# A small vision tower: recurrence on the centred stream, gates on 32 rows, third norm's gamma and beta folded into weights

## The chip, the cores and the metric

One core of a Trainium2 chip (trn2). The time is that of the whole program on the device, in microseconds (us). It is the median of several runs; each run's time lies within a few tenths of a microsecond of the others. TensorE multiplies matrices, VectorE, ScalarE and GpSimd work on tiles in on-chip memory, and SyncE queues most transfers. GpSimd doesn't read the accumulator memory (PSUM) that TensorE writes.

## The reference

16 images of 96 x 96 x 3 are cut into 6 x 6 patches (36 positions, 576 tokens of 64 channels) and pass four layers, each with a mixing block and an expert block. Each block's output is added to the stream and normalised. Cut to what the change touches:

```
h = layernorm(h + block0_attention(h)); h = layernorm(h + block0_experts(h))

# layer 1: a linear recurrence over the 36 positions, complex, per image
u     = h @ (B * exp(gamma_log)[:, None]).T          # complex
s[t]  = lambda * s[t-1] + u[t]
h     = layernorm(h + (s @ C.T).real)

# layer 1 experts: all 8 evaluated, the best two of the router's logits weighted
for e in 8: out += combine[:, e] * (gelu(h @ w1[e] + b1[e]) @ w2[e] + b2[e])

# layer 2: top-8 attention with scores max_d(q_d + k_d), then experts:
xn     = layernorm(h) * gamma + beta                 # a norm of the expert block's own
logits = xn @ Wr + br                                # best two, softmax over them
for e in 8: y += w[:, e] * (gelu(xn @ W1[e] + b1[e]) @ W2[e] + b2[e])
```

The last layer (attention, one shared hidden layer, eight output matrices, a final norm) is not changed in what it computes.

## The kernel before

The program is written by hand: one instruction list for each engine, with semaphores between them. There is no planner; each engine does its instructions in the order in which they stand, so an instruction that waits holds up all behind it on its engine. The stream of 576 tokens lies as 128 x 288: rows 0 to 63 hold the 64 channels of the first 288 tokens (h = 0), rows 64 to 127 those of the second 288 (h = 1). Most steps run once for each half, on 64 rows of the array.

Each norm is the same sequence. TensorE adds the block's output to the centred residual in bank YB. ScalarE squares it (L1025), VectorE copies it to `centred` (XC, L1259), TensorE forms the variances (L481), ScalarE takes the root (L1030), VectorE the reciprocal (L1262, `RS`). TensorE turns and broadcasts the reciprocals over the rows (`broadcast`, L489, called in `spread`), VectorE multiplies `centred` by them into `h` (HP) in `normalise` (L1267). `idle(n, bank)` (L474) issues n products of 512 columns on zeros, whose result nobody reads; they stand where TensorE would wait.

Recurrence (TensorE L779 to L794, VectorE L1494 to L1511): `h` is projected by `lru_b1` and `lru_b2` to two banks each (L784), VectorE multiplies both by tables of cosines and sines (L1505, L1507), adds them (L1508), scans (L1509) and rotates back (L1510, L1511); TensorE projects the result into YB (L792).

Experts with all eight evaluated (layers 1 and 2), `ffn(n, src)`: `up` projects a chunk of 128 hidden columns for both halves (L521), ScalarE applies gelu with the bias (L1045), `gate` spreads the chunk's routing weight over the 128 rows by a 0/1 selector (L528), VectorE multiplies (L1339), `down` projects back (L534), and a bias product adds the output biases (L540). Layer 1 has four chunks of two experts each, layer 2 eight. The routing weights stand in bf16 in `combine_parts_T` (CT3): 64 rows, of which 0 to 31 hold the three exact parts and the mark of eight experts for h = 0, and 32 to 63 those for h = 1. Rows 64 to 127 are zero. A gate product reads all 128 rows; its selector is zero for the other half.

Selection in layer 2's attention: VectorE finds the eight best keys of each query (`topped`), replaces them by a mark (L1573, `replaced`) and masks the probabilities with it (L1578, `prob2`); TensorE turns these (L877). In between TensorE runs three blocks of seven idle products: after `late_keys_in`, after `topped` and after `top_sum`, and one after `replaced`. GpSimd subtracts and scales (L446, L453), ScalarE takes exponentials (L1147) and then loads its square-root table (L1037).

Layer 2's own norm: the reciprocals of both norms are broadcast (L489, 24 passes), two idle products follow, VectorE normalises into `xn` (L1595) and multiplies by gamma and adds beta (L1596); `ffn(2, XN)` waits for that. The router uses weights already multiplied by gamma.

## Time and profile before

| | us |
|---|---|
| median of 3 runs | 147.52 (147.13 to 147.79) |
| the profiled execution, its own time | 147.68 |
| its span, first to last instruction | 145.9 |
| TensorE busy with products (PE) | 132.4 |
| VectorE busy | 95.1 |
| ScalarE busy | 66.1 |
| GpSimd busy | 44.3 |

In the profile PE is TensorE's products, PEld its weight loads, DVE VectorE, ACT ScalarE, POOL GpSimd. L784 is line 784 of the kernel. A product in fp32 shows as two passes (two records), one in bf16 as one. "128*64 128x288" is a product on 128 rows and 64 columns of the array, streaming 288 columns. A length of a product includes the time in which the next one has already started; distances between starts tell how long the array is taken.

### The profile page before, as it was taken

To read this page: it belongs to the slowest core of one execution; us is meant where nothing else is said; L and a number is where in the kernel's file an instruction comes from. 1 tells how busy PE (TensorE), PEld (TensorE's weight loads), DVE (VectorE), ACT (ScalarE), POOL (GpSimd) and SP (SyncE) were. 2 spreads that over 40 slices of the span, in tenths; PEclk is the share of its full clock that TensorE was granted. 3 is DMA by queue.
4 is the path that set the end of the run, shared out by engine and by line. 5 is a ranking of instruction groups with operands and counts; after the bars stand their busy time and mean duration, and the time that the engine had idled before them with its cause. 6 is when DMAs were issued, how large, how long until landed. Compare 5 with 4: busy or idle time off the path is not lost.

```text
span 145.9 us, 2995 instructions
## 1 busy us (share of the span) xinstructions
PE 132.4 (91%) x1159; PEld 72.9 (50%) x1159; DVE 95.1 (65%) x301; ACT 66.1 (45%) x142; POOL 44.3 (30%) x99
## 2 busy tenths in 40 slices
PE   6999999989998996899999869998999999999960
PEld 2444566647963542554553324663454465554640
DVE  6506757799953386666778999629467477306991
ACT  3555780377601101691443006365860555568352
POOL 8819887579740000036000034000592000000000
PEclk9999999999999999999999999999999999999999
DMA  4999992000000000000020000000000000000001
GB/s 158 346 401 354 244 355 119 0 4 0 4 0 0 0 4 0 0 2 0 9 56 0 0 2 4 0 0 4 0 0 0 0 4 0 0 4 0 2 0 41
DMA packets 3830, 7.74 MB, mean 53 GB/s; under 512 B 1596, under 2 KB 1820, under 8 KB 3816
## 3 DMA queue, kind: packets, MB, share of 16 engines
q1 hardware_dynamic: 3504, 7.44, 15.5%
q8 instruction: 9, 0.15, 0.4%
q10 hardware_dynamic: 312, 0.11, 0.3%
q14 instruction: 5, 0.04, 0.1%
HBM read 7.18 MB, written 0.15 MB: 50 GB/s over the span
## 4 chain that ended last, share of the span: by engine, by line
PE 69%; DVE 23%; ACT 4%; issue 3%; DVEq 0%; ACTq 0%
PE ps L474 12%; PE ps L534 5%; PE ps L521 4%; PE ps L481 4%; PE ps L489 4%; DVE scores L1552 3%; PE ps L648 3%; DVE residual L1673 3%; PE ps L528 2%; DVE patch_sb L1665 2%; PE ps L503 2%; PE ps L693 2%; PE ps L701 2%; PE ps L605 2%; PE ps L637 2%
## 5 line engine op out<-in xcount | busy, mean ns | idle before, releaser
L474 PE MATMUL ps<-idle_operand 128*128 128x512 bf16 x123 | 34.1, 393 | 3.2 <-DVE scores L1552 1.6
L1037 ACT ACT_TABLE_LOAD x16 | 20.5, 1283 | 0.3
L474 PEld LDWEIGHTS ps<-idle_operand 128*128 128x128 bf16 x123 | 10.4, 102 | 16.9 <-issue 3.7
L1025 ACT ACTIVATE squares<-ps 128x288 f32<-128x288 f32 x7 | 2.9, 411 | 23.8 <-PE ps L792 8.4
L381 POOL CAST combine_parts_T<-combine_parts_T 64x288 f32<-64x288 bf16 x2 | 0.8, 418 | 36.7 <-DVE combine_parts_T L1287 36.7
L1259 DVE COPY centred<-ps 128x288 f32<-128x288 f32 x7 | 3.2, 456 | 11.9 <-ACT squares L1025 11.9
L1339 DVE TENSOR_TENSOR hidden_gated<-hidden,ps 128x576 f32<-128x576 f32 x12 | 8.4, 750 | 3.3 <-PE ps L528 3.3
L976 PE MATMUL ps<-weights_sb,hidden 128*128 128x256 f32 (+2 forms) x28 | 9.8, 472 | 0.0
L1045 ACT ACTIVATE hidden<-ps,weights_sb 128x576 f32<-128x576 f32 x12 | 8.5, 738 | 2.5 <-PE ps L521 2.1
L1552 DVE TENSOR_REDUCE scores<-ps 128x32 f32<-128x512 f32 (+1 forms) x13 | 7.7, 653 | 0.7 <-PE ps L844 0.7
L446 POOL TENSOR_TENSOR patch_sb<-scores,top 128x288 f32<-128x288 f32 (+1 forms) x2 | 1.6, 782 | 18.2 <-DVE top L1561 18.1
L534 PE MATMUL ps<-hidden_gated,weights_sb 128*64 128x288 f32 x48 | 6.9, 417 | 0.0
L481 PEld LDWEIGHTS ps<-consts_sb,squares 128*96 128x96 f32 x48 | 4.7, 164 | 3.9 <-ACT squares L1025 3.4
L489 PE MATMUL ps<-consts_sb,rstd 96*64 96x96 f32 x108 | 6.2, 253 | 0.1
L489 PEld LDWEIGHTS ps<-consts_sb,rstd 96*64 96x64 f32 x108 | 4.7, 136 | 2.7 <-DVE rstd L1262 2.0
L521 PE MATMUL ps<-xn,weights_sb 64*128 64x288 f32 x32 | 5.5, 446 | 0.5 <-ACT hidden L1045 0.4
L976 PEld LDWEIGHTS ps<-weights_sb,hidden 128*128 128x128 f32 (+1 forms) x28 | 4.6, 182 | 2.4 <-issue 1.6
L481 PE MATMUL ps<-consts_sb,squares 128*96 128x2 f32 x48 | 5.4, 228 | 0.1
L503 PE MATMUL ps<-h,consts_sb 128*128 128x288 f32 x14 | 5.2, 451 | 0.0
L840 PE MATMUL ps<-bconsts_sb,q_parts 128*128 128x512 bf16 (+1 forms) x13 | 4.8, 369 | 0.0
L1267 DVE TENSOR_TENSOR h<-centred,ps 128x288 f32<-128x288 f32 x6 | 2.7, 448 | 3.1 <-PE ps L489 3.1
L1262 DVE RECIPROCAL rstd<-std 96x6 f32<-96x6 f32 (+1 forms) x8 | 1.5, 192 | 4.6 <-ACT std L1030 4.6
(346 smaller groups left out, 281.1 us busy)
## 6 DMA issues: line engine op xcount, KB each, us to landing
patch_sb<-patches SPq DMA_DIRECT2D x6, 288.0 KB, 4.8
weights_sb<-weights SPq DMA_DIRECT2D x1, 717.0 KB, 14.0
weights_sb<-weights SPq DMA_DIRECT2D x1, 689.0 KB, 12.7
weights_sb<-weights SPq DMA_DIRECT2D x1, 640.0 KB, 6.8
weights_sb<-weights SPq DMA_DIRECT2D x1, 532.0 KB, 7.5
weights_sb<-weights SPq DMA_DIRECT2D x1, 512.0 KB, 10.3
weights_sb<-weights SPq DMA_DIRECT2D x1, 394.0 KB, 11.3
selectors<-sels SPq DMA_DIRECT2D x1, 384.0 KB, 9.8
```

What stands on the lines that cost most here:

```text
L474: mm(PS[:, bank, :], idle_in[:, 0:P], idle_in[:, :], start=True, stop=True)
L481: last = mm(psVar[:, 2 * t:2 * t + 2], SQ[:, cols(t)], c("mean"), start=True, stop=True)
L489: last = mm(dst[rows(h), cols(t)], RS[:, at + 2 * t + h:at + 2 * t + h + 1].to_broadcast([TT, D]), c("ident", TT)[:, 0:TT], start=True, st ...
L503: mm(psY, c(name), HP[:, :], start=True, stop=stop, skip_group_check=True)
L521: last = mm(PS[:, z + h, 0:HALF], w1[rows(h), ch, :], src[rows(h), :], start=True, stop=True)
L534: last = mm(PS[rows(h), YB, 0:HALF], w2[:, ch, :], HG[:, ch % GRING, h, :], start=False, stop=(ch == chunks - 1), skip_group_check=True)
L840: mm(out.rearrange("p (s e) -> p s e", e=D), QA[:, j * P:(j + 1) * P], cb("id2").unsqueeze(1).to_broadcast([P, keys, D]), start=True, stop ...
L976: return mm(y3(q, a, b), tok3(q, ch), wd[:, ch, a * E:b * E], start=False, stop=(ch == 1), skip_group_check=True)
L1037: act.activation(warm[:, tables[0]:tables[0] + 1], warm[:, 0:1], func)
L1045: act.activation(HR[:, at % RING, :, :], two(ZA if ch % 2 == 0 else ZB), func, bias=w(f"b1_{n}")[:, ch:ch + 1]).then_inc(S["act_out"], 1)
L1339: dve.tensor_tensor(HG[:, at % GRING, :, :], HR[:, at % RING, :, :], two(GATE_AT[n][ch]), ALU.mult)\
L1552: dve.tensor_reduce(SC[:, j, :, 8 * g:8 * g + keys].rearrange("p h s -> p s h"), PS[:, n % 4, 0:keys * D].rearrange("p (s h d) -> p s h d" ...
```

## The change

Three parts, and a renaming.

1. Recurrence. The projections read `centred` instead of `h`, straight after the variance products. The reciprocals are then broadcast to all 128 rows for each half (banks G and G+1). ScalarE copies the two parts that belong to `centred` to on-chip memory (into `KS`), and GpSimd forms `h` from them. VectorE no longer normalises here; it multiplies the rotated sum by the reciprocals (128 x 576) before the scan. The idle products stand 6 before and 4 after the residual product instead of 9 after it.
2. Gates. Each half's gate product reads only its own 32 rows of selector and routing weights.
3. Fold. beta times the first expert weights is formed by eight products of one column (on 64 rows) between the idle products of the selection, 4 before and 3 after instead of 7. ScalarE copies the result, GpSimd adds it to the bias and multiplies the weights `w1_2` (128 x 1024) by gamma. VectorE's multiplication by gamma and addition of beta goes.
4. Some semaphores of one use each are merged (`q_mid` and `q_low`, `x3_ready` and `h3_copied`, `logits3_in` and `hres_in`), with the counts adjusted.

```diff
@@ gpsimd
+            pool.wait_ge(S["xc"], 3)
+            pool.wait_ge(S["rstd_lru"], 2)
+            pool.tensor_tensor(HP[:, :], XC[:, :], KS[:, 0:HALF], ALU.mult).then_inc(S["hp"], 1)
             gates32(1)
...
+            pool.wait_ge(S["fold2_in"], 1)
+            pool.tensor_tensor(B12[:, :], B12M[:, :], w("b1_2"), ALU.add).then_inc(S["folded2"], 1)
+            pool.wait_ge(S["folded2"], 1)
+            pool.tensor_scalar(w("w1_2"), w("w1_2"), w("gam2"), None, ALU.mult).then_inc(S["folded2"], 1)
             gates32(2)
@@ tensor, gate
                     for h in range(2):
-                        last = mm(PS[:, bank + h, 0:HALF], sel[:, g, h, :], CT3[:, :], start=True, stop=True)
+                        at = slice(4 * E * h, 4 * E * (h + 1))
+                        last = mm(PS[:, bank + h, 0:HALF], sel[at, g, h, :], CT3[at, :], start=True, stop=True)
@@ tensor, recurrence
             variance(2)
-            spread(2)
             pe.wait_ge(S["w_r1"], 16)
-            pe.wait_ge(S["hp"], 3)
+            pe.wait_ge(S["xc"], 3)
             for bank, name in ((ZA, "lru_b1"), (ZB, "lru_b2")):
                 for h in range(2):
-                    last = mm(PS[:, bank + h, 0:HALF], w(name)[rows(h), :], HP[rows(h), :], start=True, stop=True)
+                    last = mm(PS[:, bank + h, 0:HALF], w(name)[rows(h), :], XC[rows(h), :], start=True, stop=True)
                 last.then_inc(S["lru_u"], 1)
+            pe.wait_ge(S["rs"], 3)
+            for h in range(2):
+                for t in range(NT):
+                    last = mm(PS[:, G + h, cols(t)], RS[:, 2 * t + h:2 * t + h + 1].to_broadcast([TT, P]),
+                              c("ident", TT)[:, 0:TT], start=True, stop=True)
+            last.then_inc(S["bc"], 1)
             pe.wait_ge(S["cen_c"], 1)
+            idle(6, MB)
+            pe.wait_ge(S["hp"], 3)
             residual("ident")
-            idle(9, MB)
+            idle(4, MB)
@@ tensor, selection
             pe.wait_ge(S["topped"], QT * HEADS)
-            idle(7, MB)
+            idle(4, MB)
+            pe.wait_ge(S["v2_ready"], 4)
+            for ch in range(E):
+                last = mm(PS[:, G, ch:ch + 1], w("w1_2", 64)[:, ch * P:(ch + 1) * P], w("bet2", 64), start=True, stop=True)
+            last.then_inc(S["fold2_mm"], 1)
+            idle(3, MB)
...
             pe.wait_ge(S["xn"], 2)
+            pe.wait_ge(S["folded2"], 2)
             ffn(2, XN)
@@ scalar
+            act.wait_ge(S["bc"], 3)
+            for h in range(2):
+                act.activation(KS[rows(h), 0:HALF], PS[rows(h), G + h, 0:HALF], ACT.Copy).then_inc(S["rstd_lru"], 1)
...
+            act.wait_ge(S["fold2_mm"], 1)
+            act.activation(B12M[:, :], PS[:, G, 0:E], ACT.Copy).then_inc(S["fold2_in"], 1)
             table(ACT.Sqrt)
...
+            act.wait_ge(S["folded2"], 1)
             hidden(2, ACT.Gelu, range(1))
@@ vector
             variance(2)
-            normalise(2, HP[:, :], "hp")
...
             link(dve.tensor_tensor(ua[:, :], ua[:, :], ub[:, :], ALU.add))
+            dve.wait_ge(S["rstd_lru"], 2)
+            link(dve.tensor_tensor(ua[:, :].rearrange("p (h n) -> p h n", h=2), ua[:, :].rearrange("p (h n) -> p h n", h=2),
+                                   two(G), ALU.mult))
             link(dve.tensor_tensor_scan(wst[:, :], rr[:, :], ua[:, :], 0.0, ALU.mult, ALU.add))
...
-            link(dve.tensor_tensor(XN[:, :], XC[:, :], psBC2, ALU.mult))
-            dve.tensor_scalar(XN[:, :], XN[:, :], w("gam2"), w("bet2"), ALU.mult, ALU.add).then_inc(S["xn"], 1)
+            dve.tensor_tensor(XN[:, :], XC[:, :], psBC2, ALU.mult).then_inc(S["xn"], 1)
```

## Rows read from the trace of the kernel before

**Rows 1.** The page: span, busy time, granted clock, and shares of the chain

```profile
span 145.9 us, 2995 instructions
...
PE 132.4 (91%) x1159; PEld 72.9 (50%) x1159; DVE 95.1 (65%) x301; ACT 66.1 (45%) x142; POOL 44.3 (30%) x99
...
PEclk9999999999999999999999999999999999999999
...
PE 69%; DVE 23%; ACT 4%; issue 3%; DVEq 0%; ACTq 0%
```

**Rows 2.** Timeline, 48-56 us (start, length, engine, line, operation, count, [idle before])

```profile
48.01 0.46 DVE L1259 COPY centred<-ps 128x288 f32<-128x288 f32 x1 [1.29 <-ACT squares L1025]
...
48.02 0.58 PEld L481 LDWEIGHTS ps<-consts_sb,squares 128*96 128x96 f32 x6 [0.56 <-ACT squares L1025]
...
48.56 0.81 PE L474 MATMUL ps<-idle_operand 128*128 128x512 bf16 x3
...
49.29 0.53 PEld L489 LDWEIGHTS ps<-consts_sb,rstd 96*64 96x64 f32 x12 [0.42 <-DVE rstd L1262]
...
50.06 0.45 DVE L1267 TENSOR_TENSOR h<-centred,ps 128x288 f32<-128x288 f32 x1 [0.84 <-PE ps L489]
...
50.66 1.24 PE L784 MATMUL ps<-h,weights_sb 64*128 64x288 f32 x8
...
51.52 0.76 DVE L1505 TENSOR_TENSOR lru_ua<-ps,rot_in_c 128x576 f32<-128x576 f32 x1 [1.01 <-PE ps L784]
...
52.98 0.76 DVE L1508 TENSOR_TENSOR lru_ua<-lru_ua,lru_ub 128x576 f32<-128x576 f32 x1
...
53.77 1.36 DVE L1509 TENSOR_TENSOR_SCAN lru_state<-decay,lru_ua 128x576 f32<-128x576 f32 x1
...
55.98 0.71 PE L792 MATMUL ps<-lru_wc,weights_sb 128*64 128x288 f32 x4 [1.45 <-DVE lru_wc L1510]
```

**Rows 3.** The same view of TensorE's weight loads, columns of 128

```profile
36.12 1.86 PEld L626 LDWEIGHTS ps<-x_slots,weights_sb 64*128 64x128 f32 x32
...
90.62 1.07 PEld L877 LDWEIGHTS ps<-consts_sb,probs 128*128 128x128 f32 x10 [0.27 <-DVE probs L1578]
```

**Rows 4.** Timeline, 94 us, ScalarE: a copy of 128x288

```profile
94.20 0.41 ACT L1152 ACTIVATE ctx_sb<-ps 128x288 f32<-128x288 f32 x1 [1.52 <-PE ps L888]
```

**Rows 5.** Groups of GpSimd by line and form (| busy, mean ns)

```profile
L411 POOL TENSOR_SCALAR decay<-decay,lru_par 128x576 f32<-128x576 f32 x1 | 1.7, 1719 | 0.0
...
L453 POOL TENSOR_TENSOR patch_sb<-patch_sb,row_stat 128x288 f32<-128x288 f32 x1 | 0.7, 672 | 0.6 <-DVE row_stat L1571 0.6
```

**Rows 6.** The chain that ended last, 106-109 us (start, length, engine, line, count)

```profile
106.32 0.49 PE ps L528 x4
...
106.81 0.48 PE ps L540 x2
...
108.66 0.60 PE ps L528 x4
```

**Rows 7.** Timeline, first expert stage, VectorE's gate multiplications

```profile
64.91 2.75 DVE L1339 TENSOR_TENSOR hidden_gated<-hidden,ps 128x576 f32<-128x576 f32 x4 [0.70 <-PE ps L528]
```

**Rows 8.** Timeline, 98-99 us: idle products, scale by gamma, first up products

```profile
98.49 0.60 PE L474 MATMUL ps<-idle_operand 128*128 128x512 bf16 x2
...
98.61 0.43 DVE L1596 TENSOR_SCALAR xn<-xn,weights_sb 128x288 f32<-128x288 f32 x1
...
99.09 1.24 PE L521 MATMUL ps<-xn,weights_sb 64*128 64x288 f32 x8
```

**Rows 9.** Timeline of TensorE, 88-92 us: idle products and transposes

```profile
88.22 1.89 PE L474 MATMUL ps<-idle_operand 128*128 128x512 bf16 x8
...
90.26 0.39 PE L474 MATMUL ps<-idle_operand 128*128 128x512 bf16 x1 [0.16 <-DVE scores_rest L1573]
...
90.63 1.31 PE L877 MATMUL ps<-consts_sb,probs 128*128 128x128 f32 x10
```

**Rows 10.** Timeline, 92.7 us: the context's short products

```profile
92.73 1.41 PE L888 MATMUL ps<-probs_T,v_blockdiag 128*32 128x40 f32 x64
```

More of the change, by code:

```diff
@@ L96 @@
 guarded
-lru_u lru_w
-k_done q_done v2_done q_hi q_rest q_mid q_low q_parts k_parts k_bcast v2_ready score_mm score_red late_keys late_keys_in top_in top_out top_sum sub2 exp2_out norm2
+lru_u lru_w rstd_lru
+k_done q_done v2_done q_hi q_rest q_act q_parts k_parts k_bcast v2_ready score_mm score_red late_keys late_keys_in top_in top_out top_sum sub2 exp2_out norm2
 prob2 prob2_t prob2_copied ctx2_done ctx2_ready
-x3_done x3_ready s3_done h3_t h3_copied exp3_in exp3_out p3_ready p3_t p3_copied0 p3_copied1
-h3_ready y3_done comb3_done wd_c logits3_T logits3_in bias3 bias3_c bias3_split hres hres_in tile3 ss
+x3_done s3_done h3_t third_in exp3_in exp3_out p3_ready p3_t p3_copied0 p3_copied1
+fold2_mm fold2_in folded2
+h3_ready y3_done comb3_done wd_c logits3_T bias3 bias3_c bias3_split hres turned3_in tile3 ss
 out_act out_dve stored""".split()
@@ L215, in tower @@
         CX = sb("ctx2_sb", [P, HALF])
+        B12, B12M = sb("b1_2_folded", [P, E]), sb("b1_2_beta", [P, E])
         XT = sb("x3_T", [P, HALF])
@@ L829, in _ @@
             idle(6, ZA + 1)
-            pe.wait_ge(S["q_low"], 1)
+            pe.wait_ge(S["q_act"], 2)
             pe.wait_ge(S["q_parts"], 1)
@@ L919, in _ @@
             residual("ident")
-            pe.wait_ge(S["x3_ready"], 1)
+            pe.wait_ge(S["third_in"], 1)
             for h in range(2):
@@ L928, in _ @@
             idle(10, ZB)
-            pe.wait_ge(S["h3_copied"], 1)
+            pe.wait_ge(S["third_in"], 2)
             for h in range(2):
@@ L994, in _ @@
             part(0, 0)
-            pe.wait_ge(S["logits3_in"], 1)
+            pe.wait_ge(S["turned3_in"], 1)
             mm(PS[:, G + 1, E:FT * E].rearrange("p (g e) -> p g e", e=E), LT[:, 0:P],
@@ L1045, in hidden @@
                     act.activation(HR[:, at % RING, :, :], two(ZA if ch % 2 == 0 else ZB), func,
-                                   bias=w(f"b1_{n}")[:, ch:ch + 1]).then_inc(S["act_out"], 1)
+                                   bias=(B12 if n == 2 else w(f"b1_{n}"))[:, ch:ch + 1]).then_inc(S["act_out"], 1)
             act.wait_ge(S["tok_w"], 16)
@@ L1130, in _ @@
             act.wait_ge(S["q_rest"], 1)
-            act.activation(q2b[:, :], qres[0:64, :], ACT.Copy).then_inc(S["q_mid"], 1)
-            act.activation(QA[64:128, :], qres[64:128, :], ACT.Copy).then_inc(S["q_low"], 1)
+            act.activation(q2b[:, :], qres[0:64, :], ACT.Copy).then_inc(S["q_act"], 1)
+            act.activation(QA[64:128, :], qres[64:128, :], ACT.Copy).then_inc(S["q_act"], 1)
             act.wait_ge(S["v2_done"], 1)
@@ L1169, in _ @@
             act.wait_ge(S["x3_done"], 1)
-            act.activation(XT[:, :], PS[:, ZB, 0:HALF], ACT.Copy).then_inc(S["x3_ready"], 1)
+            act.activation(XT[:, :], PS[:, ZB, 0:HALF], ACT.Copy).then_inc(S["third_in"], 1)
             act.wait_ge(S["h3_t"], 1)
             act.activation(HB[:, :, :].rearrange("p b d -> p (b d)"), flat2(G, PER * P, POS), ACT.Copy)\
-               .then_inc(S["h3_copied"], 1)
+               .then_inc(S["third_in"], 1)
             for h in range(2):
@@ L1192, in _ @@
             act.wait_ge(S["logits3_T"], 1)
-            act.activation(LT[:, :], PS[:, MB, 0:P + 64], ACT.Copy).then_inc(S["logits3_in"], 1)
+            act.activation(LT[:, :], PS[:, MB, 0:P + 64], ACT.Copy).then_inc(S["turned3_in"], 1)
             table(ACT.Exp)
@@ L1197, in _ @@
             act.wait_ge(S["hres"], 1)
-            act.activation(YM[0:64, 0, :, E], PS[0:64, YB, 0:D], ACT.Copy).then_inc(S["hres_in"], 1)
+            act.activation(YM[0:64, 0, :, E], PS[0:64, YB, 0:D], ACT.Copy).then_inc(S["turned3_in"], 1)
             act.activation(YM[:, 1:FT, :, E].rearrange("p (h b) d -> p h b d", b=2),
                            PS[:, YB, D:D + 2 * P].rearrange("p (b h d) -> p h b d", b=2, h=2), ACT.Copy)\
-               .then_inc(S["hres_in"], 1)
+               .then_inc(S["turned3_in"], 1)
             table(ACT.Sqrt)
@@ L1543, in _ @@
             dve.tensor_tensor(slots(qres), psQ, slots(QA), ALU.subtract).then_inc(S["q_rest"], 1)
-            dve.wait_ge(S["q_mid"], 1)
+            dve.wait_ge(S["q_act"], 1)
             dve.tensor_tensor(QB[0:64, 0:QT * P], qres[0:64, :], q2b[:, :], ALU.subtract).then_inc(S["q_parts"], 1)
@@ L1670, in summed3 @@
                 p = rows3(q)
-                dve.wait_ge(S["hres_in"], 1 if q == 0 else 2)
+                dve.wait_ge(S["turned3_in"], 2 if q == 0 else 3)
                 sync()
```

## The prediction, made before the changed kernel had run

> **What bounds the kernel now.** I read three views. The page first: TensorE is busy for 91% of the 145.9 us and holds 69% of the chain that ended last, VectorE 23% [rows 1]. That doesn't mean that TensorE work costs time one for one: many of its products are idle ones on zeros that only fill waits (`idle` in the code). So for each of the three stretches that the change touches I read the timeline, to see which wait ends last there, and the chain of waits, whose pieces give the distance from one product's start to the next. Nothing else in the kernel moves; the renamed semaphores wait for the same instructions as before.
>
> **1. Recurrence (46.8 to 57.3 us).** Before, everything hangs in one line: centred copy until 48.47, square root and reciprocal, broadcast of the reciprocals from 49.29, normalise on VectorE 50.06 to 50.51, projections from 50.66, rotation from 51.52, its sum at 52.98, scan at 53.77 [rows 2].
> Afterwards the projections wait only for the centred copy (48.47) and for the six variance products ahead of them. Those run from 48.02 to 48.56, when idle products follow [rows 2], and a change of array shape costs about 0.10 (priced in part 2). So the projections start at 48.65, 2.01 earlier, and rotation and its sum follow 2.01 earlier: rotation 49.51, sum 50.97 to 51.73. VectorE's reciprocal is done by 49.29 and isn't in their way.
> But the scale by the reciprocals now comes after the rotation, and its own line is longer. The broadcast is queued behind the projections, which hold TensorE until 49.71. It also loads 128 columns of weights instead of 64, so its 12 passes no longer run in two halves of the array at once. Loads of 128 columns in fp32 come 1.07/10 = 0.107 apart in one place and, in two row halves at once, 1.86/32 x 2 = 0.116 per half in another [rows 3]; I take 0.11. That is 49.71 + 0.10 for the shape + 0.10 for the first load + 12 x 0.11 = 51.2 us. The result is taken up about 0.2 later, as now (loads end at 49.82, normalise starts at 50.06 [rows 2]). ScalarE's two copies have 288 columns each, like the copy of 0.41 us in [rows 4]. They start about 0.35 apart: 51.4 + 0.35 + 0.41 = 52.17. VectorE, free since 51.73, waits until 52.22, multiplies (0.76, 0.79 with its link, like the sum of the same size [rows 2]) and scans at 53.01 instead of 53.77. **Gain 0.76.** Bounds: if the copies cost nothing beyond VectorE's own order, the scan starts at 51.73 + 0.05 + 0.79 = 52.57, a gain of 1.2. If the loads cost 0.13 and the copies run end to end, 0.4.
> The normalised stream for the residual moves to GpSimd: 0.67 for 128x288 [rows 5], 52.22 to 52.9. TensorE runs six idle products meanwhile, then the residual (0.6) and four more idle ones of 0.215 (0.9), so it is ready near 54.5, before the first rotated state comes (55.98 - 0.76, [rows 2]). Free; the cover is 0.7 us.
>
> **2. Gates on 32 rows.** A gate is now two products of 288 columns in bf16 one after the other, 0.49/4 = 0.122 each [rows 6]. Afterwards each half reads only its own 32 rows. In the projections two products on separate halves of 64 rows already run side by side: eight fp32 passes of 288 columns in 1.24 us, 0.155 each, while the bias product's two on the full array take 0.48, 0.24 each [rows 2, 6]. So a pair should take 0.13 instead of 0.24: 0.12 saved.
> Against it stands the change of array shape. Four gates between other full-array products take 0.49; between down products, which use 64 columns, 0.60 [rows 6]. A change of shape is therefore about 0.10. Today the gates share the full-array shape with the residual and with the bias product. On 32 rows they don't, so residual to gate, gate to bias and bias to gate are new changes.
> The Trainium skill says the same against this change: "Mode switching requires drain" (TensorEngine Tiling (Array Packing), Tiling Modes). By that page alone every gate of a stage would be bracketed by two pauses; the rows give each of them a price, 0.10.
> First expert stage: the first gate starts 0.10 later and its pair is 0.12 shorter. VectorE then multiplies four times without a pause [rows 7] and sets the rest, so the gain is 0.02.
> Second expert stage, along TensorE's queue [rows 6]: gate 1 is done 0.02 earlier. Gate 2 saves 0.12, bias and gate 3 lose 0.10 + 0.10 and gain 0.12, so the down products start 0.04 late. Gates 4 and 5 save 0.12 each at an unchanged number of shape changes: 0.08 earlier after gate 4, 0.20 at the next down products, 0.32 when gate 6 is done. From there VectorE's last two multiplications and the last down product follow. **Gain 0.31 here, 0.33 in all.** Bounds: a loss of 0.4 if the pairs don't overlap (four new changes of shape on the path and nothing saved), a gain of 0.5 if the changes cost half.
>
> **3. Gamma and beta folded.** Removed: one VectorE instruction of 0.43 ahead of the third stage [rows 8]. It hides less than its length. Without it the stream is ready when that one begins now, 98.6, but TensorE's two idle products start at 98.49 and last until 98.93, and with the change of shape the first up product can't start before 99.03. It starts at 99.09 now. Gain 0.06. The router behind it comes 0.43 earlier, but its result is picked up by TensorE only after the fifth up product, so this brings nothing.
> Added: eight fp32 products of one column on 64 rows, between the idle products of the selection. Here the idle products are not free filler. Eight of them take 1.89 us from 88.22 on, of which the last alone shows 0.39: (1.89 - 0.39)/7 = 0.215 apart, so TensorE has no pause until 88.22 + 8 x 0.215 = 89.94 [rows 9]. The next event is at 90.26, when VectorE's replacements are done, and the transposes start at 90.63 [rows 9]. The slack is 0.32, plus 0.15 because the last idle product needn't wait.
> An fp32 product is two passes with a load each. For a single column the load sets the pace: the six variance passes, 96 columns loaded for 2 streamed, take (48.56 - 48.02)/6 = 0.09 each, the first being dearest [rows 2]. In proportion that is 0.12 for 128 columns, and rows 3 give 0.107 and 0.116. I take 0.112. All eight use the same 64 rows, so none run side by side: 16 x 0.112 = 1.79, plus two changes of shape, 0.19. The idle products stay seven in number (4 + 3), so these 1.98 us come on top: the second block now ends at 89.94 + 1.98 = 91.92, the single idle product at 92.15, and the transposes start there instead of at 90.63. That is 1.52 late; their first load is no longer exposed, which gives about 0.03 back. **Loss 1.49, net of the gain above 1.43.** Probabilities, context, output projection and everything behind follow one another from the transposes, so nothing takes it up. Bounds: 1.8 if a pass costs 0.13. The shortest rows of products show 64 in 1.41 us, 0.022 each, on four column groups [rows 10]; at that the block costs 0.35 + 0.19 and the loss is near zero.
> The copy on ScalarE delays its table load and square-root warm-up to about 91.7; its next work, the copy of the probabilities, comes after 93. GpSimd scales 1024 columns: 1.72 us for 576 [rows 5] makes 3.1, from about 90.6 to 93.7, while the first up product comes near 100.5, so 6 us of cover. All free.
>
> **Sum.** -0.76 - 0.33 + 1.43 = +0.34. The profiled execution took 147.68, 1.78 more than its span, and stands 0.16 above the median of 147.52, inside the runs' spread. 147.52 + 0.34 = 147.86.
>
> **Rivals.** (a) The fold is nearly free: short products run at the pace of [rows 10], the late transposes vanish. For it: those rows, and TensorE looks idle here. Against it: the variance passes, with two columns, already cost 0.09. Then -0.76 - 0.33 + 0 - 0.06 = -1.15: 146.4. 12%. The Trainium skill (TensorEngine Tiling (Array Packing), Instruction Overhead) would have it so: a product with a free dimension of 1 has the latency of one with 60, about 60 cycles. By that page 16 passes are an estimate of 0.4 us and the loss of part 3 is about nothing; the rows of the variance speak against it. (b) Slower: pairs on 32 rows run one after the other. No row here shows products on 32 rows. Price: +0.1 in the first expert stage and +0.3 in the second instead of -0.33, decided by whether two starts of one pair lie 0.12 or under 0.02 apart. 147.86 + 0.73 = 148.6. 14%. (c) The recurrence brings what VectorE alone allows, 1.2: 147.4. 10%. (d) The stretch of one-column products lets the granted clock fall; the page shows full clock throughout [rows 1], through a TensorE pause of 1.45 us too [rows 2]. The eleven idle products behind would cost 0.22 more each: 150.2. 3%.
>
> **Chances.** Forecast 61%, its own range 147.3 to 148.4. The range reaches from 146.8 to 148.7, which takes in (b), (c) and most mixtures and leaves out (a) and (d). A difference of 0.5% (0.74 us) is about what this kernel's measurement can tell: faster 0.14, within 0.60, slower 0.26.
>
> **What would show it.** Projections 2 us earlier but the scan only 0.6 to 0.9 earlier, with VectorE waiting for ScalarE's copies; pair starts within 0.02 and a pause of 0.1 around each pair; 16 passes some 0.11 apart near 88 us and transposes waiting for nothing but TensorE's queue. It is wrong if the passes come under 0.05 apart, or if the transposes still wait for VectorE.

## The result, and the profile after

The changed kernel takes 147.70 us (median of 22 runs, 147.04 to 150.29) against 147.12 for the kernel before, timed beside it (22 runs, 146.66 to 147.94). The ratio is 1.0035, 95% interval 1.0019 to 1.0051: 0.5 us slower. The interval lies above 1, so the sign is clear, and the size is 0.35%. The ratios here leave out two executions far above the rest of their kernel, 150.29 us of the changed kernel and 153.21 us of e8.

The page of the changed kernel, to be read against [rows 1]:

```profile
span 145.6 us, 3027 instructions
...
PE 133.1 (91%) x1171; PEld 74.0 (51%) x1171; DVE 94.7 (65%) x300; ACT 67.1 (46%) x145; POOL 49.0 (34%) x102
...
PEclk9999999999999999999999999999999999999999
...
PE 72%; DVE 18%; ACT 5%; issue 2%; DVEq 0%; ACTq 0%
```

VectorE's share of the chain fell from 23% to 18% and TensorE's rose from 69% to 72%. Most of this is the selection: there the chain ran over VectorE until 21.75 us behind the fifth square, and now it passes to TensorE's own queue at 18.41 (below). The span is 0.3 us shorter than before's although the median is 0.6 longer. The two profiled executions differ by 0.6 us before the third norm, where nothing was changed. So spans are no measure here. I compare the distances between ScalarE's squares, which open every norm. Before, as the timeline of ScalarE has them (start, length, engine, line, operation):

```profile
47.56 0.41 ACT L1025 ACTIVATE squares<-ps 128x288 f32<-128x288 f32 x1 [1.45 <-PE ps L775]
...
68.47 0.41 ACT L1023 ACTIVATE squares<-ps 128x288 f32<-128x288 f32 x1 [2.53 <-PE ps L534]
95.45 0.41 ACT L1025 ACTIVATE squares<-ps 128x288 f32<-128x288 f32 x1 [0.84 <-PE ps L894]
113.11 0.41 ACT L1025 ACTIVATE squares<-ps 128x288 f32<-128x288 f32 x1 [5.10 <-PE ps L534]
```

and the same rows of the changed kernel:

```profile
46.95 0.41 ACT L1048 ACTIVATE squares<-ps 128x288 f32<-128x288 f32 x1 [1.46 <-PE ps L785]
...
67.12 0.41 ACT L1046 ACTIVATE squares<-ps 128x288 f32<-128x288 f32 x1 [2.63 <-PE ps L544]
95.58 0.41 ACT L1048 ACTIVATE squares<-ps 128x288 f32<-128x288 f32 x1 [0.84 <-PE ps L916]
112.85 0.41 ACT L1048 ACTIVATE squares<-ps 128x288 f32<-128x288 f32 x1 [4.82 <-PE ps L544]
```

These are the third, fifth, sixth and seventh of eight squares. From the third on there are five distances (68.47 - 47.56 is two of them, 9.83 and 11.07), and behind the last square the tail, to the start of the last instruction; together they are all of the program that the change touches. I read the same rows for every experiment:

| us | recurrence | first experts | attention 2 | second experts | layer 3 | tail | sum less before's | ratio, 95% interval |
|---|---|---|---|---|---|---|---|---|
| before | 9.83 | 11.07 | 26.99 | 17.66 | 11.18 | 21.54 | | |
| after | 9.20 | 10.97 | 28.46 | 17.27 | 11.19 | 21.56 | +0.38 | 1.0035 (1.0019 to 1.0051) |
| e1 recurrence only | 9.20 | 10.98 | 27.00 | 17.65 | 11.18 | 21.90 | -0.36 | 0.9982 (0.9958 to 1.0006) |
| e2 gates only | 9.83 | 11.05 | 27.01 | 17.31 | 11.19 | 21.57 | -0.31 | 0.9962 (0.9941 to 0.9982) |
| e3 fold only | 9.83 | 11.07 | 28.46 | 17.61 | 11.19 | 21.54 | +1.43 | 1.0129 (1.0092 to 1.0165) |
| e4 no filler | 9.20 | 10.97 | 28.09 | 17.27 | 11.19 | 21.56 | +0.01 | 0.9961 (0.9932 to 0.9990) |
| e5 fold early | 9.20 | 10.97 | 27.61 | 17.27 | 11.19 | 21.56 | -0.47 | 0.9939 (0.9913 to 0.9965) |
| e6 scale before copies | 9.00 | 10.97 | 28.45 | 17.27 | 11.19 | 21.54 | +0.15 | 1.0035 (1.0006 to 1.0063) |
| e7 bias behind gates | 9.20 | 10.97 | 29.00 | 17.16 | 11.19 | 21.55 | +0.80 | one run, 147.23 us |
| e8 fold twice | 9.20 | 10.97 | 31.93 | 17.27 | 11.19 | 21.54 | +3.83 | 1.0268 (1.0233 to 1.0303) |
| f1 no fold | 9.20 | 10.96 | 27.06 | 17.31 | 11.19 | 21.91 | -0.64 | 0.9960 (0.9940 to 0.9979) |
| f2 no fold, ordered | 9.01 | 10.95 | 26.97 | 17.21 | 11.19 | 21.91 | -1.03 | 0.9944 (0.9919 to 0.9968) |
| f3 all, ordered | 9.00 | 10.96 | 26.98 | 17.17 | 11.18 | 21.56 | -1.42 | 0.9917 (0.9891 to 0.9943) |
| g1 f2, one fewer on VectorE | 9.01 | 10.96 | 27.35 | 17.20 | 11.19 | 21.55 | -1.01 | 0.9900 (0.9865 to 0.9936) |

What was changed repeats to 0.02 us in the profiles. The times of one kernel spread by 0.8 us and more all the same. One source is seen in the attention column: in some executions the score products wait for the transfer of the keys and start 0.4 to 0.6 us later (e5, e7, g1; shown at e5). The sums come from one execution of each kernel. For the changed kernel +0.38 lies inside the interval of the times (+0.28 to +0.75 us).

**Where the time went.** Timeline of the changed kernel in the recurrence (against [rows 2]):

```profile
47.39 0.46 DVE L1290 COPY centred<-ps 128x288 f32<-128x288 f32 x1 [1.29 <-ACT squares L1048]
...
48.01 1.24 PE L793 MATMUL ps<-centred,weights_sb 64*128 64x288 f32 x8
...
49.18 1.41 PEld L798 LDWEIGHTS ps<-consts_sb,rstd 96*128 96x128 f32 x12 [0.38 <-issue]
...
50.80 0.83 ACT L1141 ACTIVATE ks<-ps 64x288 f32<-64x288 f32 x2 [2.41 <-PE ps L798]
51.73 0.76 DVE L1540 TENSOR_TENSOR lru_ua<-lru_ua,ps 128x576 f32<-128x576 f32 x1 [0.64 <-ACT ks L1141]
51.78 0.80 POOL L439 TENSOR_TENSOR h<-centred,ks 128x288 f32<-128x288 f32 x1 [10.79 <-ACT ks L1141]
52.52 1.36 DVE L1542 TENSOR_TENSOR_SCAN lru_state<-decay,lru_ua 128x576 f32<-128x576 f32 x1
```

This execution stands 0.61 us earlier than before's. From the third square the projections start 1.06 us later instead of 3.10, 2.04 earlier; the scan starts 5.57 later instead of 6.21, only 0.64 earlier. The 0.64 us in which VectorE waits for the copies is the wait that took the place of the one removed. The chain has the second of the two copies by itself:

```profile
51.23 0.41 ACT ks L1141
```

The chain of waits of the changed kernel through the fold (start, length, engine, line, count), against [rows 9]:

```profile
85.58 1.04 PE ps L483 x4
86.62 1.87 PE ps L887 x16
88.49 2.48 PE ps L483 x11
90.97 1.11 PE ps L899 x10
```

Idle products, the sixteen one-column passes, eleven more idle products, transposes: TensorE's own queue without a gap. Before, the transposes waited for VectorE; now VectorE is done 1.2 us before they start.

### The profile page after: what moved, and what is told of

It is laid out like the page before. It is cut to its first block, busy times and chain, and to the rows that moved or that the text cites. A ratio compares the mean times of both kernels' runs of the same rounds, so it can differ in the third digit from the quotient of the medians.

```text
span 145.6 us, 3027 instructions
## 1 busy us (share of the span) xinstructions
PE 133.1 (91%) x1171; PEld 74.0 (51%) x1171; DVE 94.7 (65%) x300; ACT 67.1 (46%) x145; POOL 49.0 (34%) x102
## 4 chain that ended last, share of the span: by engine, by line
PE 72%; DVE 18%; ACT 5%; issue 2%; DVEq 0%; ACTq 0%
PE ps L483 14%; PE ps L544 5%; PE ps L530 4%; PE ps L490 4%; PE ps L498 3%; DVE scores L1585 3%; PE ps L658 3%; DVE residual L1705 3%; DVE patch_sb L1697 2%; PE ps L512 2%; PE ps L711 2%; PE ps L615 2%; PE ps L703 2%; PE ps L647 2%; PE ps L538 2%
## 5 line engine op out<-in xcount | busy, mean ns | idle before, releaser
L483 PE MATMUL ps<-idle_operand 128*128 128x512 bf16 x119 | 33.1, 393 | 3.0 <-DVE scores L1585 1.6
L1068 ACT ACTIVATE hidden<-ps,b_folded 128x576 f32<-128x576 f32 x8 | 5.8, 739 | 2.0 <-PE ps L530 1.7
L498 PE MATMUL ps<-consts_sb,rstd 96*64 96x96 f32 x96 | 5.5, 253 | 0.1
L498 PEld LDWEIGHTS ps<-consts_sb,rstd 96*64 96x64 f32 x96 | 4.2, 136 | 2.3 <-DVE rstd L1293 1.7
L1053 ACT ACTIVATE std<-ps,eps 96x6 f32<-96x6 f32 x8 | 2.1, 261 | 5.3 <-PE ps L490 5.3
```

The lines of the kernel that those rows point to most:

```text
L483: mm(PS[:, bank, :], idle_in[:, 0:P], idle_in[:, :], start=True, stop=True)
L498: last = mm(dst[rows(h), cols(t)], RS[:, at + 2 * t + h:at + 2 * t + h + 1].to_broadcast([TT, D]), c("ident", TT)[:, 0:TT], start=True, st ...
L1068: act.activation(HR[:, at % RING, :, :], two(ZA if ch % 2 == 0 else ZB), func, bias=(B12 if n == 2 else w(f"b1_{n}"))[:, ch:ch + 1]).then_ ...
```

## The experiments

**One part at a time.** e1 is the kernel before with the recurrence's lines of the diff alone, e2 with the gates' alone, e3 with the fold's alone. All three have the merged semaphores of part 4 as well.

```diff
 e1, against before: tensor; copies, GpSimd's product and the scaling as in part 1
-            spread(2)
...
-                    last = mm(PS[:, bank + h, 0:HALF], w(name)[rows(h), :], HP[rows(h), :], start=True, stop=True)
+                    last = mm(PS[:, bank + h, 0:HALF], w(name)[rows(h), :], XC[rows(h), :], start=True, stop=True)

 e2, against before
+                        at = slice(4 * E * h, 4 * E * (h + 1))
-                        last = mm(PS[:, bank + h, 0:HALF], sel[:, g, h, :], CT3[:, :], start=True, stop=True)
+                        last = mm(PS[:, bank + h, 0:HALF], sel[at, g, h, :], CT3[at, :], start=True, stop=True)

 e3, against before: tensor; bias and scaling of the weights as in part 3
-            idle(7, MB)
+            idle(4, MB)
+            pe.wait_ge(S["v2_ready"], 4)
+            for ch in range(E):
+                last = mm(PS[:, G, ch:ch + 1], w("w1_2", 64)[:, ch * P:(ch + 1) * P], w("bet2", 64), start=True, stop=True)
+            last.then_inc(S["fold2_mm"], 1)
+            idle(3, MB)
```

> Only the recurrence part of the change; gates and fold as before. My theory (the broadcast of 12 passes and the two copies set the time of the scan): 0.64 us less than before, as the two traces show from the square ahead to the square behind (9.84 and 9.20); ratio 0.9957. Rival 1 (the stage gains only what the six idle products around it allow, so nothing): ratio 1.000. Rival 2 (VectorE alone sets it): 1.2 us less, ratio 0.992.

> Only the gates on 32 rows. Theory (pairs side by side, 0.12 saved each, about 0.10 paid for every change of shape): 0.35 to 0.5 us less, ratio 0.997; the pair starts 0.004 apart. Rival (the changes of shape eat the gain): ratio 1.000 or above. Rival on the clock (products on 32 rows let the granted clock fall in some executions): granted clocks under 1.000 and single times 1 us above the rest here, and not in the kernels without this part.

> Only gamma and beta folded. Theory (16 passes of 0.112 and two changes of shape behind full idle products): 1.45 us more than before, ratio 1.010; transposes wait for TensorE's queue alone. Rival (the fold is free and the loss of the whole change comes from somewhere else): ratio 0.999 to 1.001. Rival on the clock (one-column products let the granted clock fall in some executions): granted clocks under 1.000 and single times 1 to 3 us above the rest here, and not in the kernels without this part.

Recurrence: -0.63 in its own stage and -0.09 in the next. Gates: -0.02 and -0.35. Fold: +1.47 before the transposes and -0.05 in its expert stage. That adds up to +0.33; the changed kernel's stages show 9.20 + 10.97 + 28.46 + 17.27 = 65.90 against 65.55, +0.35. To 0.02 us the parts are independent: they share neither a gain nor a cost. e3 has the attention stage of the changed kernel, 28.46, without the other two parts, so that loss is the fold's alone. The ratio of e1 fits its stages only once its tail is seen: 21.90 instead of 21.54. I come back to this at g1.

The -0.09 behind the recurrence has its cause on ScalarE. In before it pauses ahead of the first gelu of the stage, waiting for nothing that the profile shows; in e1 and the changed kernel it doesn't. The chains of before, and then of the changed kernel:

```profile
61.10 0.21 ACT gate_col L1120
61.30 0.14 issue
61.45 0.75 ACT hidden L1045
```

```profile
59.85 0.21 ACT gate_col L1148
60.06 0.69 ACT hidden L1068
```

Counted from the fourth square, the gelu starts 4.05 us later in before, e2 and e3, where it is the 64th record on ScalarE, and 3.85 later in every kernel with the new recurrence, whose two copies make it the 66th. Of these 0.20 us 0.09 is left at the next square. No run moves the instruction without the copies, so that its place does it is not shown.

**e4, no filler.** The one-column passes take the place of the idle products instead of coming on top.

```diff
 e4, against after
-            idle(4, MB)
             pe.wait_ge(S["v2_ready"], 4)
             for ch in range(E):
                 last = mm(PS[:, G, ch:ch + 1], ...)
             last.then_inc(S["fold2_mm"], 1)
-            idle(3, MB)
@@ after top_sum
-            idle(7, MB)
+            idle(5, MB)
```

> The whole change, but the seven idle products around the fold's products are gone and the block behind has five instead of seven. Theory (the fold costs only because idle products stand in the same queue): it runs 16 x 0.112 + 0.2 = 2.0 us where 1.5 us of idle products stood, and 0.43 less of them behind, so the transposes wait for VectorE's masked probabilities again: 1.45 us less than the changed kernel, 1.1 less than before, ratio to before 0.9925. Rival (the loss comes from GpSimd's scaling of 1024 columns, or from ScalarE's later table load, which are still there): ratio stays at 1.003. Rival on the clock (fewer idle products let it fall): some executions with a granted clock under 1.000 and a median above 147.

Ratio 0.9961, and the twelve times are in two groups: six from 145.93 to 146.38 us, six from 146.79 to 147.61, the profiled one in the second. Its windows on TensorE (stretch, busy and count, granted clock) say what separates them:

```profile
86.00:87.00 1.00, 1.00 (x12) 1.00 0.06 16
87.00:88.00 1.00, 1.00 (x6) 0.61 0.00 0
88.00:90.00 2.00, 2.00 (x7) 0.50 0.00 0
```

and its chain:

```profile
85.30 1.94 PE ps L886 x16
87.24 2.66 PE ps L483 x6
89.90 1.53 PE ps L897 x10
```

Six idle products take 2.66 us, 0.44 each, where in the changed kernel eleven take 2.48, 0.225 each. Behind a stretch of one-column passes the granted clock falls from full to half, 2.4 to 1.2 GHz. This is rival (d), which I had at 3%. The first group of times, about 1.1 us below before's as forecast, is by inference the one in which the clock holds: mean clocks of the runs are 0.991 to 1.0 there and 0.979 to 0.988 in the second. With the filler in place such executions are rare: in the changed kernel one of 22 (150.29 us at a mean clock of 0.987, all others at 0.991 or more), in e3 one of 6 (150.03 us at 0.985), in e6 none of 12. So the idle products around the passes, which look like waste in the sum, mostly keep the clock. In e5 and f3 below the passes stand between score products and 21 idle ones instead, and none of their 18 executions is under 0.991. The Trainium skill says that the array's clock is gated by how busy TensorE has been (TensorE: Matmul & The Clock Gate, What's actually happening). The trace agrees in part: the clock changes with what TensorE does, but the profile's busy share doesn't tell when. TensorE is busy throughout these windows, the one ahead of the fall (86 to 87 us, in which 12 products start) included.

**e8, fold twice.** The eight products are issued twice, with the filler as in the changed kernel.

```diff
 e8, against after
-            for ch in range(E):
+            for ch in [*range(E), *range(E)]:
```

> The whole change, but the eight products of one column are issued twice, 32 passes. Theory: 16 x 0.112 = 1.79 us more in the stage from the fourth square to the fifth, 30.25 instead of 28.46; ratio to before 1.0155 where the clock holds. On the clock: 3.6 us of one-column passes in a row. If such passes don't keep the clock up, it falls to half in most or all executions, and the idle products behind take 0.43 instead of 0.216 each: 2 us more again, ratio 1.03. If they do, there is one group of times.

The stage grows by 3.47 us. The chain has the 32 passes at 3.66 us, 0.114 each as forecast, so the passes themselves explain 1.79. The rest is the clock:

```profile
86.83 3.66 PE ps L887 x32
90.48 3.70 PE ps L483 x11
94.19 1.57 PE ps L899 x10
```

Eleven idle products take 3.70 instead of 2.48, ten transposes 1.57 instead of 1.11: 1.68 together. Five of the six times lie from 150.45 to 151.23 and one is 153.21; their mean clocks are 0.975 to 0.989. So by the mean clocks a stretch twice as long lets the clock fall in every execution, although the filler stands around it.

**e5, fold early.** The same products are moved ahead of the wait for the last scores' maxima, where TensorE paused in before, ahead of 21 idle products; the filler is whole again (7 in its old place). The pause is the 1.60 us in this row of before:

```profile
85.08 5.02 PE L474 MATMUL ps<-idle_operand 128*128 128x512 bf16 x21 [1.60 <-DVE scores L1552]
```

```diff
 e5, against after
             n = len(SCORE_UNITS)
+            pe.wait_ge(S["v2_ready"], 4)
+            for ch in range(E):
+                last = mm(PS[:, G, ch:ch + 1], ...)
+            last.then_inc(S["fold2_mm"], 1)
             pe.wait_ge(S["score_red"], n)
             pe.wait_ge(S["late_keys_in"], 1)
@@ after topped
-            idle(4, MB)
-            pe.wait_ge(S["v2_ready"], 4)
...
-            last.then_inc(S["fold2_mm"], 1)
-            idle(3, MB)
+            idle(7, MB)
```

> The whole change, with the fold's eight products moved: they stand behind the last score product, where TensorE otherwise pauses for VectorE, and all three blocks of seven idle products are back. Theory (the loss is nothing but the place in TensorE's queue): 1.9 us of passes fit in the 1.99 us from the last score product to the first idle one, less 0.22 for that product itself, so the idle block starts 0.33 late and ends when VectorE's eight best keys are done; the stage from the fourth square to the fifth goes from 28.46 back to 27.0 us; ratio to before 0.9925 (1.1 less). The clock should hold as in the kernel before, so no second group of times as with the idle products taken away. Rival (one-column passes cost the clock wherever they stand, because the pause of 1.6 us is now beside them): a second group of times some 1.3 us higher, as without the idle products. Rival (GpSimd's or ScalarE's part of the fold costs): the stage stays above 28.

Ratio 0.9939, one group of times, mean clocks 0.991 or more. The timeline of TensorE has the passes under cover, and the transposes behind VectorE's last replacement again:

```profile
82.41 1.94 PE L882 MATMUL ps<-weights_sb 64*128 64x1 f32 x16
84.28 4.82 PE L483 MATMUL ps<-idle_operand 128*128 128x512 bf16 x21
89.26 0.39 PE L483 MATMUL ps<-idle_operand 128*128 128x512 bf16 x1 [0.15 <-DVE scores_rest L1605]
89.62 1.31 PE L898 MATMUL ps<-consts_sb,probs 128*128 128x128 f32 x10
```

The stage is 27.61 though, not 27.0. The missing 0.6 lies ahead of all this, in the chain of waits of the same kernel:

```profile
72.06 3.51 DMA k_parts_img<-k_parts_tok
```

The score products wait for the keys' transfer. In before and after its place in the chain is taken by idle products on TensorE. e7, whose code is the changed kernel's up to there, has the same piece of DMA (3.45 us) and the same 0.5 us, so it is a matter of the execution and not of the edit. From the first score product that reads the keys to the transposes it is 13.71 us in e5 and 13.70 in before: behind the keys the fold costs nothing.

**e6, scale before copies.** The prediction's upper bound for the recurrence was a multiplication that doesn't wait for ScalarE. VectorE reads the broadcast first, ScalarE copies behind it.

```diff
 e6, against after: vector, scalar
-            dve.wait_ge(S["rstd_lru"], 2)
+            dve.wait_ge(S["bc"], 3)
...
-            act.wait_ge(S["bc"], 3)
+            act.wait_ge(S["rstd_lru"], 1)
```

(GpSimd's wait becomes 3, and the idle products stand 9 before the residual product.)

> The whole change, with one order turned: VectorE multiplies by the reciprocals as soon as the broadcast is done, and ScalarE's two copies come behind it, beside the scan; nine idle products ahead of the residual product and none behind. Theory (the copies, 0.93 us on the path, set the scan): the multiplication starts at the end of the sum, 0.61 earlier, but the residual product, which now comes later through copies and GpSimd (0.8 each), ends near the first rotated state: the stage from the third square to the fourth shrinks from 9.20 by 0.4 to 0.6 us, ratio to before 1.0000. Rival (the residual's chain through ScalarE and GpSimd becomes the bound): no gain, 9.2 or more.

Only 0.20 of the 0.4 to 0.6 us came in the profile, and the ratio of the times, 1.0035, is no better than the changed kernel's:

```profile
51.39 0.75 DVE L1539 TENSOR_TENSOR lru_ua<-lru_ua,ps 128x576 f32<-128x576 f32 x1
52.18 0.84 ACT L1140 ACTIVATE ks<-ps 64x288 f32<-64x288 f32 x2 [3.54 <-DVE lru_ua L1539]
52.18 1.36 DVE L1542 TENSOR_TENSOR_SCAN lru_state<-decay,lru_ua 128x576 f32<-128x576 f32 x1
53.16 0.96 POOL L439 TENSOR_TENSOR h<-centred,ks 128x288 f32<-128x288 f32 x1 [11.91 <-ACT ks L1140]
53.57 1.16 DVE L1543 TENSOR_TENSOR lru_wc<-lru_state,rot_out_c 128x576 f32<-128x576 f32 x1
```

Counted from the projections, which start at 48.27 here, the scan starts after 3.91 us instead of 4.51, 0.60 earlier. Against before that makes 0.64 + 0.60 = 1.24, the bound of 1.2 that I gave. But GpSimd's multiplication now runs beside VectorE's rotation back, and both are longer: 1.16 instead of 0.76 and 0.96 instead of 0.80. f2, f3 and g1 have the same order and repeat it to 0.01 us. In the changed kernel GpSimd runs beside the scaling, which stays at 0.76 and has one operand in PSUM, and the rotation is free of it. The Trainium skill lists GpSimd's memory interfaces as shared with VectorE, with contention when a VectorE instruction has two operands there (GPSIMD Engine Reference, Specifications); L1543 has two, and the trace agrees with 0.40 us. The scan has two as well and is not longer (1.36), though GpSimd starts 0.38 before it ends. So the scan can start 1.2 us earlier than in before, and the stage gains 0.83.

**e7, bias behind gates.** The second pair's bias product goes behind all 16 gate products, so that gates 2 and 3 stand together.

```diff
 e7, against after
                     gate(2, G, 0)
-                    bias2(False)
                     pe.wait_ge(S["act_out"], BASE[2] + 8)
                     gate(3, ZB)
+                    bias2(False)
```

> The whole change, but in the third stage's experts the output bias product stands behind gate 3 instead of between gates 2 and 3. Theory (each change of array shape costs about 0.1): one change less on the path, the stage from the sixth square to the seventh goes from 17.27 to about 17.15. Rival (gate 3 waits for the eighth gelu, so nothing): 17.27.

One run; 17.16 instead of 17.27 in the stage. Chain of the changed kernel, and then of e7:

```profile
106.40 0.35 PE ps L538 x4
106.75 0.68 PE ps L550 x2
107.44 0.23 PE ps L538 x2
```

```profile
106.31 0.47 PE ps L538 x6
106.78 0.68 PE ps L550 x2
```

Six gates in a row and bias: 1.15 us; split by the bias product: 1.26. One change of array shape fewer is worth 0.11. In before the same stretch takes 1.21, the two first pieces of [rows 6] and this one:

```profile
107.29 0.24 PE ps L528 x2
```

**f1, f2, f3, g1: what the parts are worth in the best order.** f1 is the changed kernel without the fold; f2 has e6's and e7's order besides; f3 has all three parts with the orders of e5, e6 and e7. Their edits are those shown.

> The change without its third part: the recurrence projects the centred stream and the gates lie on 32 rows, gamma and beta of the third stage are multiplied in as before. If the parts add up as their single runs say, the distances from the third square on are 9.20, 10.97, 27.00 and 17.3 us, the sum of the four 0.63 + 0.10 + 0.35 = about 1.1 us shorter than before's 65.55, and the ratio about 0.993 (146.1 us against 147.1). Rival, that the parts share a gain or a cost (the 0.39 us of the fourth distance belongs partly to the shorter scaling of the fold): fourth distance 17.35 and a ratio of 0.9935. A ratio above 0.997 would say that the single runs' gains don't survive together.

> The same, with the recurrence's multiplication put ahead of the two ScalarE copies (measured: 9.00 instead of 9.20 us) and the second pair's bias product put behind the 16 gate products (measured: 17.16 instead of 17.27 us). Theory: both gains are independent, so the distances are 9.00, 10.97, 27.00 and 17.2, about 1.4 us less than before in all, ratio 0.9905 (145.7 against 147.1). Rival, from the run in which the multiplication was moved alone (its ratio 1.0035 was no better than the change's own): the 0.20 us shows in the profile and not in the time, and the ratio is that of the kernel without the fold, within 0.001.

> All three parts, with the ten one-column passes put ahead of the wait for the last scores' maxima, the multiplication ahead of the copies and the bias product behind the gates. Theory: the passes are covered there, so the third part costs nothing and brings at most 0.05 us; distances 9.00, 10.97, 27.0 and 17.16 if the keys' transfer lands as in before, 27.6 if it lands 0.6 us late; ratio 0.990 to 0.994. Rival, that the passes still hold the score products or the idle products behind them: third distance 27.6 in a profile in which the keys land early, ratio 0.994 or more, above that of the kernel without the fold. The granted clock should stay at full speed throughout, and the times should form one group.

f3 is faster than before, 145.74 us against 147.22, ratio 0.9917, and so than the changed kernel, whose ratio is 1.0035 (the two were not timed beside each other). Its passes (sixteen, not ten as the expectation has it) are hidden wholly (attention 26.98, before 26.99), and the third part brings 0.04 to 0.05 us in its expert stage (17.17 against 17.21 in f2). f1 and f2 missed: the ratios are 0.9960 and 0.9944, not 0.993 and 0.9905. Their four stages are as forecast to 0.1 us; the tail is not. It is 21.91, as in e1, and 21.54 to 21.57 in all others. In the chain of f1 the difference is one line, an engine that waits for nothing that the profile shows ("issue"):

```profile
134.97 0.40 issue
135.37 0.75 DVE residual L1693
```

e1, f1 and f2 have 341 records on VectorE, its waits included, and the second sum of this stage (L1693 in f1) is the 320th of them; in before, e2, f3 and after, with 340, it is the 319th, in e3, with 339, the 318th. g1 tests whether the place alone does it:

```diff
 g1, against f2
-            dve.memset(one3[:, :], 1.0).then_inc(S["zero3"], 1)
+            pool.memset(one3[:, :], 1.0).then_inc(S["zero3"], 1)
```

> The ordered kernel without the fold, in which one fill of a small constant tile at the very start is made by GpSimd instead of VectorE; nothing else is changed. In the three kernels without the fold but with the new recurrence VectorE has 341 entries in its list, and between the first two sums of the last stage it stands still for 0.40 us without waiting for anything; in the kernels with 340 or 339 entries the same place shows 0.04. Theory: the pause hangs on where that instruction stands in the list, so with 340 entries it is gone: from the last square to the end 21.55 instead of 21.91 us, ratio about 0.992 (146.0 against 147.2). Rival: the pause comes with what the kernel computes there or before (the scaling of the third stage's stream by gamma and beta), and stays: 21.91 us and a ratio of 0.9944, as in the run before.

```profile
134.62 0.04 issue
134.66 0.75 DVE residual L1693
```

The pause is gone (0.04), the tail is 21.55, and the ratio 0.9900. A fill of constants at the program's start, moved to another engine, takes 0.36 us from the program's end. That the pause comes and goes with one record more or fewer ahead on VectorE is shown, by g1 and by every other kernel here. It is not that any 320th record pauses: in before the 320th is a multiplication, which starts without a gap, and in e3 a wait, 0.04 us behind the record ahead of it. What the engine does in the pause no run shows. Not settled is the rival given for f2, that its orders show in the profile and not in the time: f2's ratio is 0.0016 below f1's where the sums say 0.0027, and the intervals hold either.

## Why the prediction was right, and where it wasn't

Forecast 147.9, measured 147.70; faster, same or slower was given as 0.14, 0.60, 0.26, and the ratio of 1.0035 lies within 0.5%. The working's sum of +0.34 us meets +0.38 in the profiles. Part of this closeness is luck. The forecast starts from 147.52, and the kernel before measured 147.12 beside the changed one: the start was 0.40 too high and the difference of the medians, +0.58, is 0.24 above the sum. Within the sum, 0.13 too much gain for the recurrence is offset by 0.09 that nobody forecast and by 0.04 more from the gates. By its own steps:

- **Nothing else moves.** Right for both unchanged stages (11.19, 21.56).
- **Recurrence, -0.76 forecast, -0.63 measured** (and -0.09 in the next stage, ScalarE's pause, which I had at nothing). The mechanism is the forecast one: projections 2.04 earlier for 2.01, VectorE waiting for the copies. The broadcast is right: its loads end 2.58 us behind the start of the projections (49.18 + 1.41 - 48.01), for 2.6 in the working (51.2 - 48.65). The terms mis-sized stand behind it. The copies start 0.43 apart (50.80 and 51.23) for the 0.35 taken, end to end as in the lower bound, and VectorE takes them up 0.10 later instead of 0.05. The Trainium skill's rule for a load (TensorE: Matmul & The Clock Gate, LDWEIGHTS), the number of columns over 1.2 in ns, gives 0.107; for the fold's passes it is within 0.005 of the measured 0.112.
- **GpSimd's product under cover.** Right in the changed kernel (0.80 for 0.67, cover enough). In e6 it was not free: it cost VectorE 0.40.
- **Gates, -0.33 forecast, -0.37 measured** (-0.02 in the first stage as forecast, -0.35 for -0.31 in the second). The two starts of a pair lie 0.004 apart in the trace, and the next gate starts 0.133 behind the first instead of 0.245. Rival (b) is out. Four gates between full-array products take 0.35 for 0.49, and the bias product between gates 0.68 for its two passes instead of 0.48, 0.10 more for each of the two changes around it. The Trainium skill's statement that switching the mode requires a drain (TensorEngine Tiling (Array Packing), Tiling Modes) agrees with these pauses, and they don't decide. But the working has a slip here. By its own terms the first down product of the stage comes 0.02 + 0.12 - 0.10 - 0.10 + 0.12 = 0.06 early, not 0.04 late, and the gain would be 0.41 and the whole sum +0.24. In the chain gates 1 and 2, bias and gate 3 take 0.49 + 0.48 + 0.24 = 1.21 us there and 0.35 + 0.68 + 0.23 = 1.26 in the changed kernel: 0.05 late. Three pairs save 0.11 each, so by this estimate the three new changes cost 0.13 each and not 0.10. The slip took 0.10 off the gain and the price too low by 0.03 put as much on it; that the term came out is luck.
- **Fold, +1.43 forecast, +1.42 measured** (+1.47 and -0.05). Sixteen passes with the change into them 1.87 us, starts 0.112 apart; the transposes wait for TensorE's queue alone. Rival (a) is out: a product of one column costs its load here, 0.112 us, and not the 60 cycles of the Trainium skill (TensorEngine Tiling (Array Packing), Instruction Overhead), which would be some 0.4 us for all sixteen.
- **xn, -0.06 forecast.** Right. From the sixth square to the first up product it is 3.64 before (95.45 to 99.09) and 3.58 after (95.58 to 99.16), 0.06 less, and e3's expert stage is 0.05 shorter.
- **Copies and scaling of the weights.** Right: the scaling on GpSimd took 2.85 for 3.1 and ended 6.5 us before the first up product.
- **Rival (c), 1.2 for the recurrence.** Out for the changed kernel. e6 brings the scan forward by 1.24, and 0.40 of it goes to GpSimd beside VectorE: 0.83 is left.
- **Rival (d), the clock.** This is the step that was weakest. The price of 0.22 us for each idle product was right (0.44 - 0.225). The argument for the chance was not: I argued from a page of the profile that shows full clock through a pause of TensorE, but no row of before shows a stretch of one-column products, and a row of a pause says nothing of it. It hit, by the mean clocks, one of 22 runs of the changed kernel and half of e4's. One of 22 doesn't refute the 3%, and the median didn't move. Where the filler was left out, in e4, the ratio forecast (0.9925) missed by it: 0.9961.

## What to carry to other kernels

Before a helper computation is put "between idle products", find the event that ends that wait, and count the slack; it was 0.3 us here, and the same sixteen passes cost nothing 4 us earlier in the queue. Products of one column cost their weight load (0.112 us per pass at 128 columns in fp32), and the clock can fall behind them: with 1.9 us of them between idle products it held in 38 of 40 executions by the mean clocks (the changed kernel, e3, e6), without the idle products in half. So look at more than one execution. When a stage's gain isn't found in the total, sum the distances between fixed marks; here they led to a pause of 0.36 us at the other end of the program. And when a forecast comes out, redo its terms one by one: two of them were off here and offset each other.

## What the runs showed of the hardware

- Behind 16 one-column passes without idle products around them the granted clock fell to half in the profiled execution, and by the mean clocks in six of twelve; behind 32, with idle products, by the mean clocks in all six, and the eleven idle products behind took 3.70 us instead of 2.48.
- Two products on neighbouring groups of 32 rows start 0.004 us apart. A change of array shape costs 0.10 to 0.13.
- A VectorE multiplication with both operands in on-chip memory took 1.16 us instead of 0.76 beside a GpSimd multiplication, which took 0.96 instead of 0.80.
- A pause of 0.36 us on VectorE came and went with one instruction more or fewer in its list. One of 0.14 us on ScalarE stood ahead of its 64th record and was gone where the same instruction was the 66th.
- The transfer of the keys lets the score products start 0.4 to 0.6 us later in some executions than in others whose code is the same up to there.
